# Selective stage of an eight-block network: the averaging of the chosen scores moved on VectorE to the middle of the next turn, the filter input inside the last norm, and a bias addition later on GpSimd

## The reference

```
s = q k^T / sqrt(32) over 120 context rows, 4 heads; keep the 32 largest of a row, softmax over them
a = mean of the 4 heads' weights (times the text mask);  c = a (ctx Wv)
u = layernorm(xl) * g_in + b_in;   u = u * (1 + gate * (c Wf_in)_scale) + gate * (c Wf_in)_shift
y = long convolution of u with a kernel K, + u * D_skip          (by a real Fourier transform of length 512)
y = y * (1 + gate * (c Wf_out)_scale) + gate * (c Wf_out)_shift
t = xl + y;   t = t + gelu(layernorm(t) W1 + b1) W2 + b2;   x = x + layernorm(t) * g_out + b_out
```

## Time and profile before

| | us |
|---|---|
| median of 3 runs (4632.79 to 4633.71) | 4632.93 |
| the profiled execution | 4636.67 |
| its span, first to last instruction | 4634.9 |
| busy: TensorE products, VectorE, ScalarE, GpSimd | 4151.4, 3322.0, 2232.4, 529.9 |
| the selective stage within the span | about 3521 to 4316 |
| mean granted TensorE clock over the span | 0.946 |

### The profile page before, as it was taken

The page is one execution under the profiler, slowest core; times in us unless marked ns, Lnnn a source line. Parts: engine busy times, 40 slices in busy tenths (PEclk is TensorE's granted clock), DMA queues, the critical chain, the costliest instruction groups (busy, mean ns, idle before and its releaser), DMA issues. The chain is left out here.

```text
span 4634.9 us, 72082 instructions
## 1 busy us (share of the span) xinstructions
PE 4151.4 (90%) x23376; PEld 3267.9 (71%) x23376; DVE 3322.0 (72%) x7934; ACT 2232.4 (48%) x5314; POOL 529.9 (11%) x982
## 2 busy tenths in 40 slices
PE   7998988999699999999999999999985888888686
PEld 6876766777387877778777777777863665656555
DVE  6985667666677777777777677777767888876455
ACT  3545655555365565655555555565531232322332
POOL 1331010111500000000000000001142111111300
PEclk9998999999799999999999999999975999989699
DMA  3000000000000000000000000000020000000101
GB/s 93 0 0 37 0 1 0 0 0 0 18 3 2 4 2 4 1 2 4 2 4 2 4 1 2 4 2 2 1 72 1 1 1 0 0 1 0 40 0 36
DMA packets 33797, 40.58 MB, mean 9 GB/s; under 512 B 5550, under 2 KB 30006, under 8 KB 33466
## 3 DMA queue, kind: packets, MB, share of 16 engines
q1 hardware_dynamic: 32732, 37.03, 2.7%
q10 hardware_dynamic: 800, 0.33, 0.0%
HBM read 32.90 MB, written 4.19 MB: 8 GB/s over the span
## 5 line engine op out<-in xcount | busy, mean ns | idle before, releaser
L1739 ACT ACTIVATE global_prob_t_high<-psum 128x512 fp32r<-128x512 f32 x960 | 570.7, 601 | 588.9 <-PE psum L1853 588.9
L1647 DVE TENSOR_TENSOR global_prob_t_low<-psum,global_prob_t_high 128x512 fp32r<-128x512 f32 x960 | 657.2, 690 | 251.0 <-ACT global_prob_t_high L1739 237.0
L1653 DVE TENSOR_REDUCE global_top<-psum 128x1 f32<-128x480 f32 x1024 | 666.9, 658 | 110.8 <-PE psum L1813 106.3
L1811 PE MATMUL psum<-global_prob_t_high,global_v_low 128*128 128x512 f32 x960 | 455.6, 475 | 1.0
L1811 PE MATMUL psum<-global_k_high,global_q_low 128*128 128x480 f32 x1024 | 390.6, 381 | 17.4 <-ACT spare L1760 14.8
L1813 PE MATMUL psum<-global_k_high,global_q_high 128*128 128x480 f32 x1024 | 391.1, 382 | 0.0
L1812 PE MATMUL psum<-global_k_low,global_q_high 128*128 128x480 f32 x1024 | 388.9, 380 | 0.0
L1812 PE MATMUL psum<-global_prob_t_low,global_v_high 128*128 128x512 f32 x960 | 379.7, 396 | 0.0
L1813 PE MATMUL psum<-global_prob_t_high,global_v_high 128*128 128x512 f32 x960 | 379.6, 395 | 0.0
L1760 ACT ACTIVATE spare<-psum,global_bias 128x480 f32<-128x480 f32 x512 | 337.8, 664 | 16.5 <-DVE global_bias L1656 15.1
L1760 ACT ACTIVATE global_prob<-psum,global_bias 128x480 f32<-128x480 f32 x512 | 337.9, 663 | 1.2
(11 more groups left out here) (455 smaller groups left out, 8593.3 us busy)
## 6 DMA issues: line engine op xcount, KB each, us to landing
x_res<-in_x SPq DMA_DIRECT2D x8, 512.0 KB, 9.8
moe_we<-in_expert_t SPq DMA_DIRECT2D x8, 512.0 KB, 7.6
out<-x_res SPq DMA_DIRECT2D x4, 1024.0 KB, 8.5
cho_wqkv<-in_L_ffn_Wqkv SPq DMA_DIRECT2D x2, 1536.0 KB
self_ctx_t<-in_ctx_t SPq DMA_DIRECT2D x2, 1440.0 KB, 13.6
sel_w<-in_L_xattn_W SPq DMA_DIRECT2D x2, 1024.0 KB, 11.2
global_ctx_t<-in_ctx_t SPq DMA_DIRECT2D x1, 1440.0 KB
sel_ctx_t<-in_ctx_t SPq DMA_DIRECT2D x1, 1440.0 KB
```

The costliest lines, as they stand in the source:

```text
L1647: dve.tensor_tensor(dst, psum, high.bitcast(F32), ALU.subtract).then_inc(ready.sem, 1)
L1653: ins = dve.tensor_reduce(top[:, c:c + 1], w.psum[:, c, 0:chunk], AX.X, ALU.max)
L1739: act.activation(dst, psum, ACT.Copy).then_inc(ready.sem, 1)
L1811: pe.matmul(to, lhs_low, rhs_high, start=start, stop=False)
```

## The change

On GpSimd the first power of the b half now comes ahead of the addition of b_norm_out. On VectorE `average` is called for F (the item whose scores were chosen in the iteration before) after L2508 and ahead of L2515, instead of for T after `choose`. The sum with the feed-forward output and its statistics come straight after `choose`, and the two operations on the film input follow them, ahead of the centring of the last norm.

```diff
@@ gpsimd, iteration @@
                 if now:
                     i, p = now
+                    scale_rows(pool, chain, "b", 2 * i)
                     need(pool, "xl_ready", i)
                     pool.tensor_tensor(both_tiles(i), both_tiles(i),
                                        rows["b_norm_out"][:, :].unsqueeze(1).to_broadcast([P, LANES, D]),
                                        ALU.add).then_inc(sig("x_biased").sem, 1)
-                    scale_rows(pool, chain, "b", 2 * i)
                     scale_rows(pool, chain, "b", 2 * i + 1)
@@ vector, iteration @@
                                                        rows["b_norm_in"][:, :], ALU.mult, ALU.add)
                     link(ins)
+                if F:
+                    average(F[0])
                 if now:
                     i, p = now
                     need(dve, "film_out_ready", i)
...
                 if T:
                     choose(T[0])
-                    average(T[0])
+                if now:
+                    i, p = now
+                    need(dve, "ffn_psum", i)
+                    link(dve.tensor_tensor(xt, w.psum[:, 4:6, 0:D], xt, ALU.add))
+                    dve.engine_nop().then_inc(sig("ffn_kept").sem, 1)
+                    stats("b", 2 * i + 1, lambda s: xt[:, s, :])
                 if F:
                     i, p = F
                     need(dve, "film_in_ready", i)
...
                 if now:
                     i, p = now
-                    need(dve, "ffn_psum", i)
-                    link(dve.tensor_tensor(xt, w.psum[:, 4:6, 0:D], xt, ALU.add))
-                    dve.engine_nop().then_inc(sig("ffn_kept").sem, 1)
-                    stats("b", 2 * i + 1, lambda s: xt[:, s, :])
                     centre("b", lambda s: xt[:, s, :], y, "g_norm_out")
```

## The result

The changed kernel takes 4644.23 us (median of 10 runs, 4638.44 to 4652.45) against 4633.34 us for the kernel before (10 runs, 4628.65 to 4637.71): ratio 1.0024, 95% interval 1.0015 to 1.0033. It is slower by 11 us. The execution that was profiled is the longest of the ten, 4652.45 us, against 4636.67 for the profiled one of before: 15.8 us lie between the two traces, some 5 more than between the medians.

A forecast was written before the change was run, and what follows sets the result against it. VectorE's chain was taken to bound before, the mean's path after: 13 x 43.6 + 3.6 - 605 - 7.8 + 15 c, with c = 3.7, gives +13 us, 4646 us; own range 4637 to 4661, eight in ten 4610 to 4664.

The forecast's parts named there:

- likeliest case: Whole kernel: the mean's path takes over and its pause costs the clock through the film; 4646 us, chance with D 0.50.
- Who bounds: Steady turn: VectorE bounds before; after, TensorE waits some 3.4 us for the mean, VectorE about 6 ahead of the sum.
- The turn at full clock, 43.6: Steady turn between starts of the outgoing film product, along the path through the mean: 43.6 us without clock loss.
- B: As a stretch on TensorE: turned mean to turned h, L2716 to L2731 before the change, 6.73 us at full clock.
- The clock's loss, 3.7 a turn: TensorE behind its pause for the mean: 1.2 us ahead of the film plus 2.5 in it, bounds 0 and 5.2.
- c: Clock's loss per turn on the mean's path, taken as 3.7 us, in thirteen steady turns and about two end turns.
- the rival at 4603: Clock loss by the Trainium skill's figure, only 0.8 us a turn: near 4603 us, chance 0.08 of the faster rival's 0.28.
- The loop ends, 0.7 each: Five loop ends on VectorE: 1.64 us each, partly hidden behind GpSimd, leaves 0.7 each, 3.6 us in all.
- The ends: Turns outside the thirteen: first -5.3, second -3.6, last with a film +1.1 us; clock loss in about two of them.
- B (the clock stays up): Rival at L2716 to L2731: clock stays up or returns before the film, c under 2.2; 4591 to 4609 us, chance 0.28.
- C (no difference): Rival, whole kernel: c between 2.2 and 3.5, saved waits and lost clock cancel, -9 to +9 us; chance 0.22.
- D: Rival, slower still: all of the incoming film at 0.50, c = 5.2, +36 us (4669); chance with the likeliest case 0.50.

The follow-up runs named there:

- the two runs on GpSimd's order: Kernel before with the first b power ahead of the b_norm_out addition, 4630.35 us; changed kernel with GpSimd's old order, 4650.96 us.
- the cut version: Changed kernel with masking, sums and reciprocal put back behind `choose`, only the weighting of the heads left in the next turn: 4569.62 us, ratio 0.9879.

## Why the prediction was right

4646 us was forecast, on the median of before; 4644.23 was measured. Its likeliest case, slower by the clock's loss on the mean's path, is the one that came, and the runs bear out its mechanism: the averaging's place makes the whole loss, and the fill of the pause takes it back. The closeness of the total is in part luck, as its terms show. They are taken from the profiled executions, which lie 15.8 us apart, where the medians lie 10.9.

**Who bounds.** Right. VectorE's wait ahead of the sum was to be about 6 us and is 79.0/13 = 6.1; the waits for the exponentials and the filter are gone; TensorE's wait for the mean was to be some 3.4 and is 3.2 on the mean. L2499 takes 0.69 and the update of x 0.88 a pair, as said.

**The turn at full clock, 43.6.** The profiled turn from 3723.21 to 3770.43 (starts of L2538) is 47.22; without what B is over 6.73, 10.64 - 6.73 = 3.91, it is 43.3. The 0.3 over is mostly GpSimd: its power was to end last by 0.9, and VectorE waits only 0.27 for it. Against the forecast this is -3.9 us in 13 turns.

**The clock's loss, 3.7 a turn.** B is 9.90 on the mean of 13 turns, so c is 9.90 - 6.73 = 3.17. Somewhat less than the 3.7 taken, in place as described: 0.50 from 3742.8 to 3752.5. The part ahead of the film came as taken (3743.28 to 3747.17 = 3.89, where 3.91 was read); the film lost less than its 2.5 on the mean. Against the forecast this is -6.9 us in 13 turns. The rule of the Trainium skill, "TensorE: Matmul & The Clock Gate", section "HAM oscillation — how this bites in real kernels", that such a loop drops the clock in every turn, agrees with the trace. Its figure, some 1.67 us of slow running each, doesn't: 9.7 us are slow here and 3.2 are lost, so the rival at 4603 fell.

**The loop ends, 0.7 each: this term was mis-sized.** The thirteen turns took 618.2 us by the starts of L2538 (3630.49 to 4248.69). 618.2 - 13 x 43.3 - 13 x 3.17 = 14.1, which is 2.8 at each of the five ends. The prediction let VectorE's "issue" of 1.64 pass partly behind GpSimd. It measures 12.8/5 = 2.57 now, and GpSimd hides only the 0.27 for which VectorE waits in the other turns, which leaves 2.3. Another 0.4 is a gap ahead of L2460 in each of these five turns (0.51 in the turn at 3790), which the prediction did not have. Against the forecast +10.5 us.

**The ends.** The last turn with a film is 41.36 us (4248.69 to 4290.05), before 37.09: +4.3 where +1.1 plus its share of c, 3.7, was said. All the ends together were to be -7.8 + 2 x 3.7 = -0.4, and are 14.3 - (618.2 - 605) = +1.1.

So -3.9 - 6.9 + 10.5 cancel to about nothing.

**Rivals.** B (the clock stays up) did not come, but its price was right: with the clock held up by three products the kernel takes 4601 us. Three of the thirteen turns still had a long B there, c = 0.5 on the mean, for which the forecast's sum gives 4598. C (no difference) asked for c between 2.2 and 3.5, and c = 3.17 is inside, as it is inside the forecast's own 3.1 to 4.7: by the clock alone the total would be -42.4 + 15 x 3.17 = +5. The loop ends, which the sum had too low, put the kernel over the bound; the forecast was right with a clock loss somewhat too high and these too low. D did not come; no B reached 6.73 + 5.2.

**What the prediction did not see.** First, it treated the gain as one sum: it never asked whether the sum first without the averaging is better than both together. It is, by some 40 us. Behind L2508 the averaging fills a time in which VectorE would wait, but TensorE then stands still for its result.

Second, it read the kernel before from its best turn. The turn at 3734 is 43.50 us long (starts of L2543, 3726.05 to 3769.55), the shortest of the thirteen, and the only one in which the pause of 1.79 left the backward transform at full length: 3.72 us there, 4.3 to 5.2 in the other turns with a pause of 1.6 to 1.8, up to 5.7 at the loop ends. The evidence for rival B, that this pause did no harm, was that exception. B itself was 8.3 to 8.4 us in four of the thirteen turns of before, with 3.7 to 3.8 us of waiting for the exponentials in place of 2.1 to 2.3. So the mean of 46.5 held losses by the clock, and at full clock, loop ends aside, the two orders are nearly level: 43.5 and 43.3.

Third, the normalised input of the feed-forward block, L2427 from `spare`, grew from 0.41 to 0.73 us each since GpSimd's addition now runs beside it (3746.83 to 3748.11 by GpSimd's timeline, the pair from 3747.22 to 3748.58). In the changed kernel it harms nothing, since TensorE comes to the turned h only at 3753.92. That the addition is the cause is shown by the two runs on GpSimd's order: the longer time goes with it from L2499 to L2427 and back. The Trainium skill, "SBUF — State Buffer", section "Who interferes with whom", says that the form of that operation (one input from SBUF, by scalars) can contend with GpSimd as well as one with two inputs; the trace agrees with both, 0.41 to 0.73 and, for L2499, 0.69 to 1.04.

Open: why "issue" at a loop end grew from 1.64 to 2.57 us on VectorE was not tried, nor was the gap ahead of L2460; and what makes the clock stay up in most turns of the cut version and fall in six of fifteen was not settled.

## What to carry to other kernels

Before a step is moved off the engine that bounds, follow its result to the next engine: if that one has to stand still for it, what stands behind the pause can run at half clock. Here 3.2 us lost in each turn ate more than the gain, which was 2.1 us a turn with the loop ends counted (46.5 to 44.4, of which a part was itself the clock's loss in the kernel before). A cheap test whether a pause costs clock is to fill it with products that nobody reads: three turned a loss of 11 us into a gain of 31, one did nothing. And read several turns of the kernel before, not one: the turn that is easiest to read may be the one in which nothing goes wrong. Last, a step is not one piece: cut in two, with the larger part left where VectorE has the time, it gave 60 us (4629.23 to 4569.62) where moving the whole lost 11.

## What the runs showed of the hardware that was not expected

- In the changed kernel's turn at 3743 the clock is 0.98 over nearly all of the pause (3739.8 to 3742.7) and 0.50 after it, for 9.7 us, through products that keep TensorE busy for 8.06 of them; the price falls on what follows.
- One product of 1.12 us, with 2.42 us of pause left, does not keep the clock up (B 10.2 on the mean); three, with 0.70 left, do in 12 of 15 turns.
- Two products that fill the pause ahead of the turned tile (1.79 us in the turn of the earlier trace rows) gave the kernel before 12 us, though the turned tile's products looked undisturbed in the turns with that pause (0.66 us for four): the loss was in the backward transform behind them (468 to 408 ns on the mean).
- A GpSimd addition of 128x512 lengthened a tensor-tensor operation of VectorE of the same size from 0.69 to 1.04 us and one with a single tensor input (L2427) from 0.41 to 0.73; moving the addition moved the price.
- "Issue" at a loop end is not a constant of the loop: 1.64 us where VectorE came late, 2.57 where it came early.
